# A Mamba-2 stage on Trainium2: dt and the skip term's D move from the operand x into the decay mask

## The reference

```python
zxbcdt = x @ W_in.T
z, xBC = zxbcdt[..., :256], zxbcdt[..., 256:768]
dt = softplus(zxbcdt[..., 768:] + dt_bias)          # 4 heads
xBC = silu(causal_conv4(xBC) + conv_b)
xs, Bm, Cm = xBC[..., :256] (4 heads x 64), xBC[..., 256:384], xBC[..., 384:]
dA = exp(dt * -exp(A_log))
state = state * dA_t + dt_t * outer(B_t, x_t)       # step by step over 128 tokens
y_t = state @ C_t
y = y + Dskip * xs
y = rmsnorm(y * silu(z), norm_w) @ W_out.T
```

## Time and profile before

| | |
|---|---|
| time, median of 3 runs | 4106.53 us (4106.15 to 4109.89) |
| the profiled execution | 4106.24 us, its span 4104.5 us |
| busy: PE, PEld, DVE, ACT, POOL | 3875.4, 3012.2, 3014.3, 2846.5, 1809.5 us |
| share of the span | 94%, 73%, 73%, 69%, 44% |
| granted TensorE clock, mean | 0.987 |

### The profile page before, as it was taken

The page is one execution under the profiler, slowest core; times in us unless marked ns, Lnnn a source line. Parts: engine busy times, 40 slices in busy tenths (PEclk is TensorE's granted clock), DMA queues, the critical chain, the costliest instruction groups (busy, mean ns, idle before and its releaser), DMA issues. The chain is left out here.

```text
span 4104.5 us, 107091 instructions
## 1 busy us (share of the span) xinstructions
PE 3875.4 (94%) x34248; PEld 3012.2 (73%) x34248; DVE 3014.3 (73%) x7587; ACT 2846.5 (69%) x6420; POOL 1809.5 (44%) x1728
## 2 busy tenths in 40 slices
PE   8999899999979999898999989999999989998999
PEld 5677678888746666685666677888888867776777
DVE  7888665555569999658999955777777767776665
ACT  6666555555569999757999965777777767775333
POOL 3333222222268888526777753333333321112443
PEclk9999999999999999999999999999999999999999
DMA  0000100000000000100000010000000000000000
GB/s 18 9 10 9 48 8 6 6 6 6 22 28 8 8 8 8 27 17 10 8 8 8 14 29 27 1 0 0 0 0 0 0 3 3 3 3 6 12 12 13
DMA packets 109259, 42.48 MB, mean 10 GB/s; under 512 B 91232, under 2 KB 107872, under 8 KB 108512
## 3 DMA queue, kind: packets, MB, share of 16 engines
q1 hardware_dynamic: 109152, 41.10, 3.9%
HBM read 20.16 MB, written 4.19 MB: 6 GB/s over the span
## 5 line engine op out<-in xcount | busy, mean ns | idle before, releaser
L1138 POOL TENSOR_TENSOR l_rc<-l_rc,l_rs 128x1024 f32<-128x1024 f32 x128 | 303.7, 2373 | 201.5 <-DVE l_rs L1330 199.8
L1205 ACT ACTIVATE l_prob<-l_prob,l_mx 128x128 f32<-128x128 f32 x1024 | 311.9, 389 | 0.0
L1816 POOL TENSOR_TENSOR mb_steps<-w_upto,mb_dta 128x1024 f32<-128x1024 f32 x64 | 121.5, 1898 | 354.4 <-DVE mb_dta L2073 354.4
L707 POOL TENSOR_TENSOR ca_prob<-ca_prob,ca_sm 128x1232 f32<-128x1232 f32 x64 | 144.0, 2250 | 299.3 <-DVE ca_sm L873 299.3
L1230 PE MATMUL l_qk_ps<-w_local,l_hT 128*128 128x512 f32 x512 | 248.9, 609 | 12.5 <-DVE l_rs L1330 9.3
L1132 POOL TENSOR_TENSOR l_prob<-l_prob,l_sm 128x1024 f32<-128x1024 f32 x128 | 243.0, 1898 | 16.9 <-DVE l_sm L1316 16.9
L1115 POOL TENSOR_TENSOR l_rc<-l_rc,l_ss 128x1024 f32<-128x1024 f32 x128 | 243.6, 1903 | 12.5 <-POOL l_rc L1138 4.5
L1973 PE MATMUL mb_x_ps<-w_wx,mb_xT 128*128 128x256 f32 x1024 | 236.9, 384 | 0.0
L1325 DVE TENSOR_REDUCE l_ss<-l_sq 128x16 f32<-128x1024 f32 x128 | 156.1, 1219 | 77.7 <-ACT l_sq L1169 77.1
L2532 POOL TENSOR_TENSOR mo_hid<-mo_hid,mo_gate 128x1024 f32<-128x1024 f32 x64 | 121.8, 1903 | 199.8 <-DVE mo_hid L2678 199.8
L1973 PEld LDWEIGHTS mb_x_ps<-w_wx,mb_xT 128*128 128x128 f32 x1024 | 190.0, 191 | 23.2
(11 more groups left out here) (354 smaller groups left out, 12156.9 us busy)
## 6 DMA issues: line engine op xcount, KB each, us to landing
la_xin<-in_x SPq DMA_DIRECT2D x64, 64.0 KB
l_h<-lt_y SPq DMA_DIRECT2D x128, 32.0 KB
lt_quad<-lt_y SPq DMA_DIRECT2D x32, 128.0 KB
out_x<-k_x SPq DMA_DIRECT2D x64, 64.0 KB, 1.5
l_h<-lt_y SPq DMA_DIRECT2D x128, 31.8 KB
lt_quad<-lt_y SPq DMA_DIRECT2D x32, 127.0 KB
ca_ctxT<-in_ctx_T SPq DMA_DIRECT2D x128, 19.2 KB
wr_state<-in_p_state SPq DMA_DIRECT2D x1, 2438.5 KB, 11.9
```

The source lines that it names most:

```text
L1138: gp.tensor_tensor(wide(rc[l][:]), wide(rc[l][:]), wide(rs[l][:]), ALU.add).then_inc(*pool_sum.did("rot"))
L1205: ex = sc.activation(p[:, a, j], p[:, a, j], ACT.Exp, bias=mx[l][:, a, j:j + 1])
```

## The change

The factor dt_s and the skip term leave the operand x and go into the mask: with gdt[s, t] = G[s, t] dt_s + D (where s = t), the masked matrix is decay by gdt, and its product with xs itself is all of y. On the diagonal the decay is 1, so D comes through unchanged. GpSimd makes gdt per head (128x1024) in two instructions, the product of gm and dt and the addition of `ddiag`. TensorE's matmuls with `ddiag` go, and GpSimd's `xdt`.

```diff
@@ -1734,7 +1734,7 @@
         pre = both(m, "pre", [DS, NSH, T])
         zs = both(m, "zs", [128, DIRS * PAIRS, T])
         steps = both(m, "steps", [T, HEADS, T])
-        gm, xdt = both(m, "gm", [T, DIRS, T]), both(m, "xdt", [T, DIRS, DI])
+        gm, gdt = both(m, "gm", [T, DIRS, T]), both(m, "gdt", [T, HEADS, T])
         decay = both(m, "decay", [T, HEADS, T])
         u, usq = both(m, "u", [128, DIRS * PAIRS, T]), both(m, "usq", [128, DIRS * PAIRS, T])
         uq = both(m, "uq", [128, DIRS, T])
@@ -1767,7 +1767,7 @@
         pe_out = Stage(m.sem("pe_out"), "out")
         pool_norm = Stage(m.sem("pool_norm"), "xp xr")
         pool_dt = Stage(m.sem("pool_dt"), "steps")
-        pool_seg = Stage(m.sem("pool_seg"), "xdt")
+        pool_seg = Stage(m.sem("pool_seg"), "gdt gd")
         pool_out = Stage(m.sem("pool_out"), "uq")
         NORM, TURN, PROJ, SEG, OUT = range(5)
         ORDER = [*SHIFTED, *[c for c in ((0, 0), (0, 1), (1, 0), (1, 1)) if c not in SHIFTED]]
@@ -1802,13 +1802,13 @@
                                          ).then_inc(*pool_out.did("uq"))
                     b = at(SEG)
                     if b:
-                        heads = lambda ap: ap.rearrange("p k (h e) -> p (k h) e", e=HD)
-                        gp.wait_ge(*act_proj.at("sx", b))
                         gp.wait_ge(*vec_dt.at("dt", b))
-                        gp.wait_ge(*pe_seg.at("y", b, ago=2))
-                        gp.tensor_tensor(heads(xdt[b.lane][:]), heads(xs[b.lane][:]),
-                                         dt[b.lane][:].unsqueeze(2).to_broadcast([T, HEADS, HD]), ALU.mult
-                                         ).then_inc(*pool_seg.did("xdt"))
+                        gp.wait_ge(*vec_seg.at("gm", b))
+                        gp.wait_ge(*vec_seg.at("m", b, ago=2))
+                        gp.tensor_tensor(by_dir(gdt[b.lane][:]), per_head(gm[b.lane][:]), per_step(dt[b.lane][:]), ALU.mult
+                                         ).then_inc(*pool_seg.did("gdt"))
+                        gp.wait_ge(*pool_seg.at("gdt", b))
+                        gp.tensor_tensor(gdt[b.lane][:], gdt[b.lane][:], ddiag[:], ALU.add).then_inc(*pool_seg.did("gd"))
                     b = at(PROJ)
                     if b:
                         gp.wait_ge(*vec_dt.at("dta", b))
@@ -1984,14 +1984,11 @@
                         te.wait_ge(*act_proj.at("sx", b))
                         te.wait_ge(*vec_seg.at("m", b))
                         te.wait_ge(*vec_out.at("u", b, ago=1))
-                        te.wait_ge(*pool_seg.at("xdt", b))
                         place = lambda h: y_ps[64 * (h % 2):64 * (h % 2) + 64, T * (h // 2):T * (h // 2) + T]
                         cols = lambda h: slice(HD * (h % NH), HD * (h % NH) + HD)
                         for pair in range(HEADS // 2):
                             for h in (2 * pair, 2 * pair + 1):
-                                te.matmul(place(h), xdt[l][:, h // NH, cols(h)], decay[l][:, h], start=True, stop=False)
-                            for h in (2 * pair, 2 * pair + 1):
-                                mm = te.matmul(place(h), xs[l][:, h // NH, cols(h)], ddiag[:, h], start=False, stop=True)
+                                mm = te.matmul(place(h), xs[l][:, h // NH, cols(h)], decay[l][:, h], start=True, stop=True)
                         mm.then_inc(*pe_seg.did("y"))
                     b = at(TURN)
                     if b:
@@ -2027,11 +2024,11 @@
                 def decayed(b):
                     l = b.lane
                     v.wait_ge(*act_seg.at("decay", b))
-                    v.wait_ge(*vec_seg.at("gm", b))
-                    v.tensor_tensor(by_dir(decay[l][:]), by_dir(decay[l][:]), per_head(gm[l][:]), ALU.mult
+                    v.wait_ge(*pool_seg.at("gd", b))
+                    v.tensor_tensor(decay[l][:], decay[l][:], gdt[l][:], ALU.mult
                                     ).then_inc(*vec_seg.did("m"))
 
-                def softplus(b, seg):
+                def softplus(b):
 
                     row = lambda n: dts[b.lane][:, n]
                     taps = iter([(back, i) for back in range(1, TAPS) for i in range(NSH)])
@@ -2048,8 +2045,6 @@
                     v.tensor_tensor(row(5), row(2), row(4), ALU.mult).then_inc(*vec_dt.did("z"))
                     v.wait_ge(*vec_dt.at("z", b))
                     v.tensor_tensor(row(6), row(5), row(5), ALU.mult).then_inc(*vec_dt.did("z2"))
-                    if seg:
-                        decayed(seg)
                     beside()
                     v.wait_ge(*vec_dt.at("z2", b))
                     v.tensor_scalar(row(7), row(6), coefficient(TERMS), None, ALU.mult).then_inc(*vec_dt.did(f"p{TERMS}"))
@@ -2065,6 +2060,7 @@
                     v.tensor_scalar(row(3), row(0), 0.0, None, ALU.max).then_inc(*vec_dt.did("relu"))
                     beside()
                     v.wait_ge(*vec_dt.at("relu", b))
+                    v.wait_ge(*pool_seg.at("gdt", b, ago=2))
                     v.scalar_tensor_tensor(out=dt[b.lane][:], in0=row(7), scalar=2.0, in1=row(3), op0=ALU.mult, op1=ALU.add
                                            ).then_inc(*vec_dt.did("dt"))
                     beside()
@@ -2111,8 +2108,8 @@
                                                op0=ALU.mult, op1=ALU.min).then_inc(*vec_dt.did("av"))
                     b = at(PROJ)
                     if b:
-                        softplus(b, at(SEG))
-                    elif at(SEG):
+                        softplus(b)
+                    if at(SEG):
                         decayed(at(SEG))
                     b = at(PROJ)
                     if b:
```

## The result

| | before | after |
|---|---|---|
| time, median of 4 runs each on one chip | 4106.78 us (4106.15 to 4109.89) | 4465.87 us (4465.45 to 4466.48) |
| ratio, 95% interval | | 1.0872 [1.0858, 1.0885] |
| the profiled execution, its span | 4106.24, 4104.5 us | 4466.48, 4464.8 us |
| granted TensorE clock, mean | 0.987 | 0.938 |

What follows compares the result with a forecast made beforehand. It took VectorE, with TensorE also near its limit, to end each step; 63 steps of 4.1 us waits plus 1.3 us clock, plus 3.5 us once, made 344 us on 4106.24: 4450 us, range 4335 to 4500.

Steps and rivals of the forecast that it cites:

- the likeliest case: VectorE instructions wait for GpSimd's products and the idle lets TensorE's clock fall: 4450 us, chance 0.56.
- the 16.3 and 17.6 us named as signs: Predicted length of a step in the changed profile: about 16.3 us at full clock, 17.6 with the clock falls.
- Term 1: From gm to the first tap: small softplus rows on VectorE wait for GpSimd's gdt and gd, +2.2 us a step.
- Term 2: From the first convolution tap to dta: no GpSimd work beside it, 2.81 us as before.
- Term 3: From dta to k_x: the decay product, now behind the last tap, waits for GpSimd's steps, +1.9 us a step.
- the once-paid 3.5 us: In the last step, with SEG alone, gd precedes the decay product: +3.5 us once.
- the rival in which the clock holds: The stalls come as worked out but TensorE stays at 2.4 GHz: 4368 us, chance 0.30.
- Term 4: TensorE idles before and behind y, its clock falls and slows transpose, seg and g: +1.3 us a step, bounds 0 and 2.0.
- TensorE's saving counted as nothing: The 16 dropped y passes, 0.98 us a step, win no time because TensorE is not late for the step's end.
- only the long product waits: Small softplus rows slip in and only the decay product waits for GpSimd's steps: 4226 us, chance 0.05.
- no waiting: No VectorE instruction waits for GpSimd and the step stays as long as before: 4107 us, chance 0.03.
- the faster one: No waiting, VectorE's tail 0.9 us shorter a step and TensorE able to follow: 4050 us, chance 0.03.

Runs made afterwards that it cites:

- the moves alone: The kernel before with r moved ahead of gm and, on ScalarE, silu of z and the rstd pair each put ahead of its neighbour: 4107.6 us, ratio 1.0001.

## Why the prediction was right

The time lies 16 us above the point and inside the range; the likeliest case is the one that came. The profiled execution is 360 us longer, where the sum had 344. A part of the nearness is luck: the waits came out 0.1 us a step below the sum and the clock 0.3 to 0.4 above it.

- **The step it read** was the shorter of two that take turns: 11.99 us, where the mean was 12.24. The terms are differences within a step and don't depend on it; the 16.3 and 17.6 us named as signs fit the mean (12.24 and 4.1, and 1.3 more), and 16.23 and 17.93 were measured.
- **Term 1** (gm to the first tap): 2.2 us predicted. gm ends at 3016.41, the first tap starts at 3021.50: 5.09 where it was 3.02, +2.07. Both waits came as worked out, the unproven one of the 8-column tensor_scalar included (2.16). The rms product won its race in every step (210 ns in the median, 221 at most). The 0.13 us over is the gap between gdt and gd: 0.20 assumed from L1823, 0.07 measured.
- **Term 2**: 2.82 us from the first tap's start to dta's end, 2.81 before.
- **Term 3** (dta to k_x): +1.9 predicted; dta's end at 3024.32 to k_x's end at 3029.39 is 5.07 where it was 3.23, +1.84. The product ended 1.09 behind steps, 1.08 predicted.
- Terms 1 and 3 with the once-paid 3.5 us make the rival in which the clock holds: 262 us predicted; the loss without the clock's part is 258 (359 less 101). A step's waits average 3.99 us where 4.1 were predicted.
- **Term 4** (the clock): +1.3 a step predicted, 82 us; measured 101 us, 1.60 a step over the run and 1.70 in the stretch above. This is the term that was mis-sized, and the step of it that failed is the share: it counted the fall in three steps in four. In TensorE's timeline of the changed kernel seg's four L1920 passes take 1.79 to 2.07 us in every step from 2600 to 3600 us, where they take 1.03 to 1.13 at full clock, so the fall was in all of them. What it counted for one fall, 1.75 us, held: that in every step is close to the 1.60 to 1.70 measured. The clock of the stage was 0.81 (2600 to 3300 us), below the 0.9 named as a sign.
- **TensorE's saving counted as nothing**: shown; the kernel before without the ddiag matmuls measures 1.000. But the sentence that VectorE ends a step was half of it. With the moves alone the kernel before stays at 4107.6 and TensorE is busy 98% of 2600 to 3300 us; only with the matmuls gone as well does the time fall, by 17 of the 62 us (0.98 x 63) that they are worth at most. So TensorE limits the step too once VectorE's tail is shorter. How much of the tail's gain went instead in av's longer wait, no run tells.
- **Gd's price**: 2373 ns from L1138, 2352 measured. The Trainium skill, "GPSIMD Engine Reference", section 3.1, gives one figure for two inputs, by which both products would take an estimated 2.22 us; the rows show 1.90 for the one whose inputs are repeated and 2.35 for two full tiles.

The rivals: that only the long product waits (4226 us) is refuted by av and L2041, and no waiting and the faster one by the same rows. The price that the first of them gave is met by the version with the small rows in PSUM, 4226.4 us, in which the long product's wait is what is left; to the microsecond that is luck, since two rows were added there and the clock of the stage was 0.99.

The waits themselves are shown, not argued: the same product with the same data takes 2.88 us with two SBUF inputs and 1.22 with one. The Trainium skill, "SBUF — State Buffer", section "Who interferes with whom", states that a VectorE instruction with at most one SBUF input, outside its two-port modes, does not contend with GpSimd; the traces agree, 2.88 against 1.22 us and 1.40 against 0.17.

## What to carry to other kernels

Before work is moved to GpSimd, list what VectorE issues while it runs, and mark every instruction with two SBUF inputs and every tensor_scalar from SBUF. Here each of these that met one of GpSimd's tensor products or sums on the chain waited for its end, even at 128x8, and one in a dependent chain can cost nearly GpSimd's whole duration (2.16 of 2.35 us). Keeping one operand in PSUM takes the wait away; here that was 359 us, the clock's part included. When two engines are both near the bound, a saving on one can measure as nothing until the other's tail is shortened as well, so test such edits in pairs.

## What the runs showed of the hardware

- TensorE's clock fell with less idle than the earlier trace rows let expect. There an idle of 2.4 us kept 1.00. With 2.27 us before y and 0.93 behind its 1.09 us of work, the stage had 0.91; with some 2.3 us before y, 0.93; with 1.5 us before y, 0.99; with matmuls put into the idle, 1.00. In the version without the skip term's addition and in those with the decay product or the small rows in PSUM, some 0.9 us more were idle behind y. No run changes the idle before y and keeps the idle behind it, or the other way round.
- GpSimd began an instruction that waited for its own last one 0.07 us behind a 1024-column one (L1811), and 0.20 behind a 128-column one (L1823).
- A 128x8 instruction waits for the whole rest of GpSimd's: L2041 took 2.16 us for 0.17 us of work.
